# A graph network's last pass: splits 14 pieces ahead, four chunks' layers from parts, other row order

## The reference, cut to what matters

```python
def mlp(x, W1, b1, W2, b2, W3, b3):            # leaky_relu with slope 0.01 after each layer
    ...
x = layernorm(x + relu(adj @ x @ K + bias))    # pass 0
u = x
for _ in range(3):
    v = mlp(adj @ u, *uv)                      # passes 1, 3, 5
    u = mlp(adj @ v, *vu)                      # passes 2, 4 (the last u is not needed)
x = layernorm(x + v)
```

## Time and profile before

| | us |
|---|---|
| median of 3 runs | 1169.38 (1169.24 to 1169.6) |
| the profiled execution | 1169.33 |
| its span in the profile | 1167.5 |
| TensorE busy | 1153.9 |
| VectorE busy | 737.0 |
| ScalarE busy | 660.1 |
| GpSimd busy | 3.3 |

### The profile page before, as it was taken

The page is one execution under the profiler, slowest core; times in us unless marked ns, Lnnn a source line. Parts: engine busy times, 40 slices in busy tenths (PEclk is TensorE's granted clock), DMA queues, the critical chain, the costliest instruction groups (busy, mean ns, idle before and its releaser), DMA issues.

```text
span 1167.5 us, 13724 instructions
## 1 busy us (share of the span) xinstructions
PE 1153.9 (99%) x5242; PEld 953.5 (82%) x5242; DVE 737.0 (63%) x889; ACT 660.1 (57%) x813; POOL 3.3 (0%) x8
## 2 busy tenths in 40 slices
PE   7999999999999999999999999999999999999997
PEld 6888888888888888888888888888888888887876
DVE  7997676458555555555545746553566555678984
ACT  7765555346554555555444754554556544667874
POOL 0000000000000000000000000000000000000001
PEclk9999999999999999999999999999999999999999
DMA  9988775568366646555656736555564656589871
GB/s 383 403 308 321 246 271 193 204 216 288 120 207 215 213 154 212 204 191 180 211 186 216 246 115 220 205 183 184 196 237 166 212 190 225 173 296 359 309 269 36
DMA packets 72353, 261.60 MB, mean 224 GB/s; under 512 B 8032, under 2 KB 8800, under 8 KB 71264
## 3 DMA queue, kind: packets, MB, share of 16 engines
q1 hardware_dynamic: 72144, 260.61, 63.0%
q10 hardware_dynamic: 144, 0.13, 0.0%
HBM read 258.61 MB, written 2.10 MB: 223 GB/s over the span
## 4 chain that ended last, share of the span: by engine, by line
PE 94%; DMA 3%; DVE 2%; ACT 0%; SPq 0%; issue 0%; ACTq 0%
PE agg_ps L923 28%; PE agg_ps L916 28%; PE agg_ps L909 28%; PE pre_ps L820 4%; DMA adj_raw<-in_adj 3%; PE hid_ps L781 1%; PE hid_ps L783 1%; PE hid_ps L782 1%; DVE adj_lo L761 1%; PE hid_ps L842 1%; PE hid_ps L856 0%; ACT adj_hi L628 0%; DVE stats L641 0%; SPq L490 0%; PE hid_ps L859 0%
## 5 line engine op out<-in xcount | busy, mean ns | idle before, releaser
L761 DVE TENSOR_TENSOR adj_lo<-adj_raw,adj_hi 128x1024 fp32r<-128x1024 f32 x464 | 548.1, 1221 | 224.6 <-ACT adj_hi L628 219.2
L909 PE MATMUL agg_ps<-adj_hi,feat_hi 128*128 128x512 f32 x1484 | 586.4, 395 | 7.3 <-ACT adj_hi L628 7.3
L916 PE MATMUL agg_ps<-adj_hi,feat_lo 128*128 128x512 f32 x1484 | 579.2, 390 | 0.0
L628 ACT ACTIVATE adj_hi<-adj_raw 128x1024 fp32r<-128x1024 f32 x464 | 467.6, 1051 | 82.2 <-PE agg_ps L923 69.1
L923 PE MATMUL agg_ps<-adj_lo,feat_hi 128*128 128x512 f32 x1484 | 459.0, 391 | 0.2 <-DVE adj_lo L761 0.2
L909 PEld LDWEIGHTS agg_ps<-adj_hi,feat_hi 128*128 128x128 f32 x1484 | 279.4, 188 | 65.8 <-issue 9.2
L916 PEld LDWEIGHTS agg_ps<-adj_hi,feat_lo 128*128 128x128 f32 x1484 | 279.5, 188 | 59.3 <-issue 1.9
L923 PEld LDWEIGHTS agg_ps<-adj_lo,feat_hi 128*128 128x128 f32 x1484 | 278.8, 188 | 59.9 <-DVE adj_lo L761 1.5
L522 ACT ACTIVATE hid<-hid_ps,params 128x512 f32<-128x512 f32 (+2 forms) x82 | 55.2, 673 | 61.3 <-PE hid_ps L783 50.7
L593 ACT ACTIVATE in_hi<-part 128x512 fp32r<-128x512 f32 x24 | 15.2, 634 | 110.4 <-DVE part L750 110.4
L522 ACT ACTIVATE post<-pre 128x512 f32<-128x512 f32 x39 | 24.7, 633 | 88.0 <-DVE pre L728 88.0
(11 more groups left out here) (80 smaller groups left out, 389.4 us busy)
## 6 DMA issues: line engine op xcount, KB each, us to landing
adj_raw<-in_adj SPq DMA_DIRECT2D x472, 512.0 KB, 5.6
adj_raw<-in_adj SPq DMA_DIRECT2D x8, 1024.0 KB, 8.1
resid<-in_x SPq DMA_DIRECT2D x8, 256.0 KB, 8.0
out<-resid SPq DMA_DIRECT2D x7, 256.0 KB, 5.2
params<-in_weights SPq DMA_DIRECT2D x1, 386.0 KB, 4.9
b_row<-in_bias_rows SPq DMA_DIRECT2D x1, 128.0 KB, 5.4
out<-resid SPq DMA_DIRECT2D x2, 64.0 KB, 1.7
out<-resid ACTq DMA_DIRECT2D x1, 128.0 KB, 2.0
```

Of the source, the lines that this page charges most:

```text
L628: act.activation(split_hi(b)[:, i * CHUNK:(i + pieces) * CHUNK], adj_raw[:, h % RAW, 0:pieces * CHUNK], ACT.Copy).then_inc(adj_hi_ready, 1)
L761: dve.tensor_tensor(split_lo(b)[:, slot], adj_raw[:, h % RAW, 0:pieces * CHUNK], split_hi(b)[:, slot].bitcast(F32), ALU.subtract).then_inc ...
L909: pe.matmul(group_bank(g), feat_hi[feats][:, tile(src, i)], split_hi(b)[:, piece(i)], start=start, stop=False)
L916: pe.matmul(group_bank(g), feat_lo[feats][:, tile(src, i)], split_hi(b)[:, piece(i)], start=False, stop=False)
```

## The change

It does six things, all in the last pass. Splits are due 14 pieces ahead and not 20. The first four units (40 to 43) get a new row of steps, `LAST_PARTS`, with hidden layers from parts and TensorE's steps six pieces behind the VectorE step that they need. The rows of blocks come in the order 6, 1, 5, 4, 3, 2 and not 6, 5, 4, 3, 1, 2, so unit 43 is row 1, and units 44, 45, 46 are rows 5, 4, 3. The steps of `LATE2` and `LATE` move. Unit 47's bias product stands later, and its two tiles are normalised on GpSimd and not on ScalarE. The condition of the `dve_in` and `dve_hid` steps, the counts of GpSimd's waits and the slices of the moments follow from these.

```diff
-LEAD, FIRST_LEAD, LAST_LEAD, FIRST_ROWS = 12, 4, 20, 3
+LEAD, FIRST_LEAD, LAST_LEAD, FIRST_ROWS = 12, 4, 14, 3
...
+    LAST_PARTS: dict(dve_sum=0, act_in=3, dve_in=4, pe_hid1=10, act_hid1=11, dve_hid=13, pe_hid2=19, act_hid2=20,
+                     pe_out=24, dve_pre=24, act_post=27, dve_stats=28, act_std=31, dve_shift=32, act_norm=35),
     LAST: dict(dve_sum=0, act_in=0, pe_hid1=6, act_hid1=7, pe_hid2=10, act_hid2=11, pe_out=14, dve_pre=14,
                act_post=16, dve_stats=16, act_std=20, dve_shift=20, act_norm=24),
-    LATE2: dict(dve_sum=0, act_in=1, pe_hid1=4, act_hid1=5, pe_hid2=7, act_hid2=8, pe_out=9, dve_pre=10,
-                act_post=10, dve_stats=12, act_std=14, dve_shift=15, act_norm=16),
+    LATE2: dict(dve_sum=0, act_in=0, pe_hid1=5, act_hid1=6, pe_hid2=9, act_hid2=10, pe_out=13, dve_pre=13,
+                act_post=14, dve_stats=15, act_std=18, dve_shift=18, act_norm=22),
     LATE: dict(dve_sum=0, act_in=1, pe_hid1=1, act_hid1=2, pe_hid2=3, act_hid2=5, pe_out=5, dve_pre=7, act_post=7,
-               dve_front=8, dve_total=8, dve_stats=12, act_std=17, dve_root=18, pool_norm=18),
-    END: dict(dve_sum=0, act_in=0, pe_hid1=1, pe_bias=5, act_hid1=3, pe_hid2=5, act_hid2=7, pe_out=9, act_post=10,
-               dve_stats=15, act_std=19, dve_shift=21, act_norm=24),
+               dve_front=8, dve_total=8, dve_stats=9, act_std=12, dve_root=13, pool_norm=13),
+    END: dict(dve_sum=0, act_in=0, pe_hid1=1, act_hid1=3, pe_hid2=5, act_hid2=7, pe_bias=7, pe_out=8, act_post=10,
+               dve_stats=15, act_std=19, dve_root=20, pool_norm=20, act_out=24),
...
-LAST_ROWS = (6, 5, 4, 3, 1, 2)
+LAST_IN_PARTS = 4
+LAST_ROWS = (6, 1, 5, 4, 3, 2)
...
-            return END2 if after < 0 else END if after == 0 else LATE if after == 1 else LATE2 if after == 2 else LAST
+            return END2 if after < 0 else END if after == 0 else LATE if after == 1 else LATE2 if after == 2 \
+                else LAST_PARTS if u < self.rows * (PASSES - 1) + LAST_IN_PARTS else LAST
...
-                    if plan.steps_of(u) == END:
-                        act.wait_ge(act_normed, normed_by(u, False))
-                        act.dma_start(out[chunk_of(u)][:, own(u)], resid[:, columns_of(u)]).then_inc(out_written, 16)
+                u = at(t, "act_out", (LAST,))
+                if u is not None:
+                    act.wait_ge(pool_normed, normed_on_pool(u))
+                    act.dma_start(out[chunk_of(u)][:, own(u)], resid[:, columns_of(u)]).then_inc(out_written, 16)
...
                 if u is not None:
+                    tiles = slice(*plan.units[u][2])
                     dve.wait_ge(std_ready, norms(u) + 1)
-                    dve.reciprocal(moments(u)[1], std[:, :]).then_inc(rstd_ready, 1)
+                    wait_for_normed(dve, plan.first_of(u) - 1)
+                    dve.reciprocal(moments(u)[1][:, tiles], std[:, tiles]).then_inc(rstd_ready, 1)
...
-                u = at(t, "dve_hid", HIDDEN)
+                u = at(t, "dve_hid", DEEP)
...
-                u = at(t, "dve_in", HIDDEN)
+                u = at(t, "dve_in", DEEP)
```

More of the change, by code:

```diff
@@ L40 @@
 HOLD = 3
-LEAD, FIRST_LEAD, LAST_LEAD, FIRST_ROWS = 12, 4, 20, 3
+LEAD, FIRST_LEAD, LAST_LEAD, FIRST_ROWS = 12, 4, 14, 3
 LOAD_GCN, LOAD_PARAMS = 24, 90
 W_SPLIT = 320
-IN_PARTS, TURN, LATE2, LATE, END, END2 = "in_parts", "turn", "late2", "late", "end", "end2"
+IN_PARTS, TURN, LAST_PARTS, LATE2, LATE, END, END2 = "in_parts", "turn", "last_parts", "late2", "late", "end", "end2"
 STEPS = {
@@ L51 @@
                pe_out=12, dve_pre=12, act_post=15, dve_feat=17),
+    LAST_PARTS: dict(dve_sum=0, act_in=3, dve_in=4, pe_hid1=10, act_hid1=11, dve_hid=13, pe_hid2=19, act_hid2=20,
+                     pe_out=24, dve_pre=24, act_post=27, dve_stats=28, act_std=31, dve_shift=32, act_norm=35),
     LAST: dict(dve_sum=0, act_in=0, pe_hid1=6, act_hid1=7, pe_hid2=10, act_hid2=11, pe_out=14, dve_pre=14,
                act_post=16, dve_stats=16, act_std=20, dve_shift=20, act_norm=24),
-    LATE2: dict(dve_sum=0, act_in=1, pe_hid1=4, act_hid1=5, pe_hid2=7, act_hid2=8, pe_out=9, dve_pre=10,
-                act_post=10, dve_stats=12, act_std=14, dve_shift=15, act_norm=16),
+    LATE2: dict(dve_sum=0, act_in=0, pe_hid1=5, act_hid1=6, pe_hid2=9, act_hid2=10, pe_out=13, dve_pre=13,
+                act_post=14, dve_stats=15, act_std=18, dve_shift=18, act_norm=22),
     LATE: dict(dve_sum=0, act_in=1, pe_hid1=1, act_hid1=2, pe_hid2=3, act_hid2=5, pe_out=5, dve_pre=7, act_post=7,
-               dve_front=8, dve_total=8, dve_stats=12, act_std=17, dve_root=18, pool_norm=18),
-    END: dict(dve_sum=0, act_in=0, pe_hid1=1, pe_bias=5, act_hid1=3, pe_hid2=5, act_hid2=7, pe_out=9, act_post=10,
-               dve_stats=15, act_std=19, dve_shift=21, act_norm=24),
-    END2: dict(dve_sum=0, act_in=0, pe_hid1=4, pe_bias=5, act_hid1=6, pe_hid2=8, act_hid2=10, pe_out=12,
+               dve_front=8, dve_total=8, dve_stats=9, act_std=12, dve_root=13, pool_norm=13),
+    END: dict(dve_sum=0, act_in=0, pe_hid1=1, act_hid1=3, pe_hid2=5, act_hid2=7, pe_bias=7, pe_out=8, act_post=10,
+               dve_stats=15, act_std=19, dve_root=20, pool_norm=20, act_out=24),
+    END2: dict(dve_sum=0, act_in=0, pe_hid1=4, act_hid1=6, pe_hid2=8, act_hid2=10, pe_bias=10, pe_out=12,
                act_post=16, dve_stats=18, act_std=21, dve_norm=24),
 }
-LAST_ROWS = (6, 5, 4, 3, 1, 2)
+LAST_IN_PARTS = 4
+LAST_ROWS = (6, 1, 5, 4, 3, 2)
 END_UNITS = ((0, 2), (2, 3), (3, 4))
@@ L256, in in_parts @@
     def in_parts(self, u):
-        return self.steps_of(u) in (IN_PARTS, TURN)
+        return self.steps_of(u) in (IN_PARTS, TURN, LAST_PARTS)
     def count_in_parts(self, u):
@@ L447, in normed_by, with normed_on_pool @@
                        for i in range(u + 1))
+        def normed_on_pool(u):
+            return sum(plan.on_pool(i) for i in range(u + 1))
         def moments(u):
-            first = TILES if plan.on_pool(u) else 0
+            first = TILES if plan.steps_of(u) == LATE else 0
             return mean_var[:, first:first + TILES, :], rstd[:, first:first + TILES]
@@ L510, in _ @@
                 if plan.on_pool(u):
-                    sp.wait_ge(pool_normed, 1)
+                    sp.wait_ge(pool_normed, normed_on_pool(u))
                 elif plan.on_vector(u):
```

## The result

The median of the changed kernel is 1171.22 us (1170.96 to 1172.07, 22 runs) against 1169.41 (1169.17 to 1170.86, 22 runs): ratio 1.0016, 95% interval 1.001 to 1.0021. It is 1.8 us slower, which is inside the 0.2% that I called no change, but the interval leaves out 1.

A forecast was written before the change was run, and what follows sets the result against it. TensorE, busy for 1153.9 of 1167.5 us, was taken as the bound, with VectorE nearly full in the last pass. Terms from -1.5 (parts) to +1.7 (unit 46's sum) came to +1.5 us: 1170.8 us, range 1168.5 to 1172.6.

The forecast's parts named there:

- The layers from parts: Units 40 to 43, two layers each: TensorE saves 0.19 us per layer, 1.5 us in all.
- The wait for `hid_lo` of unit 42: Near piece 1475: VectorE starts this step near 1101.3, so TensorE waits about 0.5 us.
- restart: The product that follows each TensorE wait: some 0.08 us slower, 0.25 us in the sum for new waits.
- Unit 45's sum: At piece 1513: the sum starts on VectorE at 1134.6 and TensorE waits 0.5 to 1.0 us, taken as 0.6.
- Unit 46's sum: The sum now stands behind unit 45's total and statistics: TensorE waits 1.6 to 1.8 us, taken as 1.7, where 0.26 before.
- Unit 47's sum: Unit 46's statistics now stand between total and this sum: 1.1 us later, with TensorE waiting.
- The end: Unit 47: moved bias product -0.3 us, one `shift` row less on VectorE -0.1, tiles on GpSimd +0.1.
- The lead: Splits 14 pieces ahead, not 20: three splits, 3.4 us, move into the last pass and VectorE's queue.
- (b): Rival: VectorE's backlog grows and TensorE runs at its pace, +1 to +3 us on top, 1171.8 to 1174; chance 0.13.
- (c): Rival: GpSimd's tiles and VectorE hold each other up on the shared port, +0.8 to 1.6 us; chance 0.06.
- (d): Rival: layers from parts give nothing, +1.5 us, so 1172.2; chance 0.04.
- (a): Rival: only the gain shows, the sums aren't held up, -1.5 to 0 us, so 1167.9 to 1169.3; chance 0.13.

The follow-up runs named there:

- both orders: Changed kernel with unit 45's statistics behind unit 46's sum and unit 46's statistics behind the sums of units 47 to 49, unit 47 still on GpSimd: 1169.74 us.
- both orders, ScalarE: The both orders kernel with unit 47's two tiles normalised on ScalarE again, its bias product still moved: 1169.25 us (ratio 0.9998).

## Why the prediction was right, and where it wasn't

The forecast was 1170.8 us, no change, and 1171.2 came. Each step by its own number:

- **The layers from parts**, -1.5: 1.60 in TensorE's stream up to unit 44, and 1.35 in the medians of the pair with and without them, where a wait for ScalarE gives some of it back.
- **The wait for `hid_lo` of unit 42**, 0.5: the step from the product ahead is 1.00 us (1101.34 to 1102.34), 0.77 more than 0.227. VectorE came to it at 1101.51; the forecast was 1101.3, so with the 0.16 of the start the addition over 29.9 us of VectorE's rows was right within 0.1. What I left out was the 0.14 from VectorE's end to the product. Up to unit 44's first layer the changed kernel takes 82.04 us from 1037 us where the kernel without this wait takes 81.16, so with the slower products behind it the wait cost 0.88. With its restart of 0.08 the forecast had 0.58: this is the term that was most off.
- **Unit 45's sum**, 0.6: 0.59 with the restart (its product starts 0.82 us behind the one ahead, less 0.227), of which 0.43 is idle time. The sum started at 1134.71, forecast 1134.6. The slower product behind a wait, for which the forecast held 0.08 each, is in that number.
- **Unit 46's sum**, 1.7 + restart: 1.85 with it (2.08 less 0.227). Moving the statistics took off 1.17, and taking 4.9 us of load from VectorE took off nothing, so it comes from an order and not from a load.
- **Unit 47's sum**, +1.1: 1.11, from total to sum 1.92 instead of 0.81.
- **The end**, -0.3 for the bias product: -0.17 (2.80 against 2.97), about half. GpSimd ending with VectorE came true to 0.1 us, and moving unit 47 back to ScalarE changed nothing.
- **Not in the sum**: 0.14 us more between VectorE's end and the end of the span. The 0.1 that I had added there for GpSimd's tiles hid it by luck.
- **The lead**: here the reasoning failed, though not the sum. I let 3.4 us of splits flow into VectorE's backlog beside the 4.9 of subtractions. VectorE could have done them in the 3.46 us in which it waits at 1071.69 for ScalarE, behind unit 40's activations, so only the end of the pass (0.2) knew of the lead. I had also read the earlier trace rows too narrowly: with the waits for `feat_hi` and for output products VectorE had 9.4 us of waits there and not 5.2, which is more than the 8.3 us that I moved in. My addition came out right because it was anchored behind the wait at 1071.69.

The rivals: a backlog that grows until TensorE runs at VectorE's pace (b) didn't come, and without the parts the two big waits stand as they were; the two small ones did come with the parts' load, and went by moving steps as well. The shared port (c) showed 0.1 us in VectorE's last two rows and not 0.8 to 1.6. Parts that give nothing (d) is refuted. That only the gain shows (a) failed on a few numbers of the table of steps: with others, and with unit 47 on ScalarE, the same parts are 1.9 us ahead of the kernel before.

What is only argued: how the 0.13 us that the bias product fell short divides between ScalarE and TensorE, and what makes the end of the span come later when the last two transfers leave together.

## What to carry to other kernels

When engines take their work in program order, look for every wait of the critical engine at what stands directly ahead of the instruction that ends it, before you ask whether that engine is overloaded: here 3.5 of 3.7 us of TensorE's waits in the last pass went by changing the places of steps, with the same work; the 0.2 that are left are a new wait. A table of such places holds for one order of the blocks only; change the order, and read it through again. And price both ends of a moved step: taking the statistics off the chain gave 0.3 instead of 1.1 us because the engine that they feed had another unit's work queued behind them.

## What the hardware did that I had not expected

GpSimd and VectorE slow each other when both work on SBUF, but in no row here by the whole length of the other's instruction. VectorE's normalisation of 128x128 took 0.34 to 0.42 us beside GpSimd's tiles (0.38 and 0.42 in the changed kernel) and 0.34 or 0.35 without them. Its total of 128x128 with two SBUF inputs took 0.26 to 0.35 beside them. GpSimd's tile is 0.79 or 0.80 us in most places, and the first of unit 46's four is 1.06 with both orders, where VectorE's 128x256 total (0.43 us) starts 0.13 behind it; in the kernel before that total starts 0.22 behind it, takes 0.50, and the tile keeps its 0.80. So the four tiles take 3.38 us beside three of VectorE's totals in one kernel (both orders, ScalarE) and 3.13 beside three of them in the kernel before; what decides which of the two engines waits isn't shown. The Trainium skill ("SBUF — State Buffer", Who interferes with whom) has them lock each other out for a whole instruction; the most that a tile lost here is 0.27 us. A transfer's issue on SyncE's queue takes 0.33 us where it has time, and three in a row took 1.30 or 1.31 us. From the last issue to the end of the span 2.1 us passed where it stood 0.7 us behind the one before it (both orders, GpSimd), and 2.35 to 2.5 where the last two stood within 0.12 us.
